# Fused attention and gated FFN: where the QKV projection leaves PSUM, and where q and k are scaled

## The chip, the cores and the metric

One Trainium2 chip, one core. The metric is the time of one execution on the device in microseconds; lower is better. Engines are named as in the profile: PE (TensorE, PEld its weight loads), DVE (VectorE), ACT (ScalarE), POOL (GpSimd), SP (SyncE, which issues the DMAs here). Columns are elements of the free dimension of a tile of 128 partitions.

## The reference

Input x is 2 x 1024 x 512 in float32. All of it is float32:

```python
xn = layernorm(x)                       # no weights
q, k, v = xn @ Wq.T, xn @ Wk.T, xn @ Wv.T    # 32 q heads, 8 k/v heads, head size 128
q, k = rmsnorm(q) * q_norm_w, rmsnorm(k) * k_norm_w    # over the head's 128 elements
scores = q @ k.T / sqrt(128) + slope[head] * (key - query), masked to key <= query
s = softmax(scores) @ v, all heads side by side, @ Wo.T
g = silu(down(silu(gate(xn)) * up(xn)))      # inner size 1376
out = x + s * g
```

Four q heads share one k/v head (G = 4).

## The kernel before, in words

A **unit** is one batch and one k/v head: 2 x 8 = 16 units, in order, the function `units`. A unit has 8 row tiles of 128 tokens. PE keeps float32 accuracy by splitting each operand into a high and a low part (`_hi`, `_lo`, type float32r) and adding three products, so whatever PE multiplies is first copied by ACT (the high part) and then subtracted by DVE or POOL (the low part).

Within a unit the work goes in steps i = 0 to 7 (the last unit of a batch has two more that drain the pipeline). In step i, PE's order is written out by hand in `step` (L366): project tile i + 2 (`project`, L288), the output projection of tile i - 2 (`out_project`, L354), then slots k = 0, 1, ... Each slot may hold: one block of the scores of tile i (`scores`, L314, up to 512 keys of one head, 4 to 8 blocks per step), one turn of the probabilities of tile i - 1 through the transpose ring (`turn_probs`, L329), one weighing of v by a turned block (`weigh`, L340, two slots behind its turn), and after the last turn the transposes of q and k of tile i + 1 (`turn_q`, `turn_k`). The numbers of turns in steps 0 to 7 are 8, 1, 2, ... 7; those of score blocks are 4 in steps 0 to 3 and 8 in steps 4 to 7. The other engines have functions of the same form, in the same order of steps and slots. Every engine takes its own queue in order; semaphores tie them, with counts per tile (`tile(U, i)` = U*8 + i + 1), per score block and per ring entry.

PSUM has 8 banks: the projection takes two (`qkv_ps`), scores two (`score_ps`), the ring three (`ring_ps`), one is `out_ps`. The projection of one tile is 128 x 768 columns: 512 of q (bank one), 128 of k and 128 of v (bank two), as 12 pairs of a 512-column and a 256-column matmul (L299, L300). What happens to it:

- ACT squares q and k (`square`, L479, 640 columns out of PSUM, to `qk_sq`), then copies v to `v_nat` (`stage_v`, L485, 128 columns).
- DVE sums the squares per head (`sum_squares`, L643).
- POOL computes the inverse roots, 12 small dependent operations and one multiply (`norms`, L905, to `rq`, 5 numbers per token), then splits v (`split_v`, L915). In step 1 it makes the low part of the output weights between the two (`low_o`, L878, two operations of 1024 columns), in step 5 that of the next unit's QKV weights (`low_w`, L872, four of 768 columns, whose high parts ACT copies in slots 0 to 3 of that step, `high_w`).
- DVE multiplies q and k by `rq`, from PSUM into `natural` (`scale_qk`, L650), in slot k = 2 of the step. One operation, 640 columns.
- PE turns the result in the next step.

The two banks are free for the next projection only after v is copied and q and k are scaled: L291 and L292 wait for both. In the first steps of a batch the tiles 0 and 2 are projected into the score banks (`first_ps`), and the scores of step 1 wait for the same two (L379, L380).

DVE's slot is: `bias` of score block k (L668), `low_probs` of turn k (L685), then `scale_qk` if k is 2, then the low parts of q and k. A score block n waits until the bias of block n - 2 is done (two score banks). A step of DVE begins with `low_att` (L700), which the output projection waits for, `divide` (L691), `sum_squares` and `add_y` (L705). Output projection 2 of a unit waits besides for the first half of `o_lo` at head 0 and for the second at head 2 (L358, L359).

Of the kernel before, what the change touches and what calls it, by code (L numbers as in the profile page):

```python
# [33 lines left out]
VBUFS = 4  # L34
# [27 lines left out]
LAG = 2  # L62

# [18 lines left out]
def build(nc, x, w_qkv, w_o, w_ffn, q_norm, k_norm, rel, slopes, inv_slopes, ident_in, out):  # L82
    ctx = ExitStack()
    with ctx:
# [69 lines left out]
        qk_done, v_staged, v_high, v_split = sem("qk_done"), sem("v_staged"), sem("v_high"), sem("v_split")  # L154
# [28 lines left out]
        def tile(U, i):  # L183

            return U * TILES + i + 1

# [94 lines left out]
        def _(pe):  # L281
# [6 lines left out]
            def project(U, i, acc, early):  # L288

                if not early:  # L290
                    pe.wait_ge(qk_done, tile(U, i) - 1)  # L291
                    pe.wait_ge(v_staged, tile(U, i) - 1)  # L292
                for c in range(DC):
                    if i == 0:
                        pe.wait_ge(w_split, U * DC + c + 1)
                    for xT, w in ((xT_hi, qkv_hi), (xT_hi, qkv_lo), (xT_lo, qkv_hi)):
                        a = xT[:, c, i * P:(i + 1) * P]
                        go, end = c == 0 and xT is xT_hi and w is qkv_hi, c == DC - 1 and xT is xT_lo
                        pe.matmul(acc[:, 0:BANK], a, w[:, c, 0:D], start=go, stop=end)  # L299
                        mm = pe.matmul(acc[:, BANK:BANK + KV], a, w[:, c, D:NW], start=go, stop=end)  # L300
                mm.then_inc(projected, 1)

            def turn_q(U, i, r, first, t):
                ring_free(U, r, first)
                pe.wait_ge(qk_done, t)
                for h in range(G):
                    tr = pe.transpose(ring_ps[:, ring_bank(r), h * P:(h + 1) * P], qk[i % 2][:, h * P:(h + 1) * P], ident[:, :])  # L307
                tr.then_inc(ring_full, 1)

            def turn_k(U, i, r, first):  # L310
                ring_free(U, r, first)
                pe.transpose(ring_ps[:, ring_bank(r), 0:P], qk[i % 2][:, G * P:NQK], ident[:, :]).then_inc(ring_full, 1)  # L312
# [53 lines left out]
            def step(U, i, first, last):  # L366
                ahead = not (last and i >= TILES - 1)
                if first and i == 0:
# [6 lines left out]
                    turn_k(U, 1, RING_AT[0] + BEFORE[0] + 1, True)  # L375
# [13 lines left out]
                for k in range(slots):  # L389
# [8 lines left out]
                    if ahead and turns and k == turns + 1:  # L398
                        turn_q(U, (i + 1) % TILES, RING_AT[i] + BEFORE[i], first, tile(U, i + 1))
                        turn_k(U, (i + 1) % TILES, RING_AT[i] + BEFORE[i] + 1, first)  # L400
# [14 lines left out]
            for b in range(B):  # L415
# [41 lines left out]
                def unit(U, first, last):  # L457
                    if first:
# [8 lines left out]
                        turn_k(U, 0, 1, True)  # L467
# [10 lines left out]
        def _(act):  # L478
            def square(acc, t, first):  # L479
                act.wait_ge(projected, t)  # L480
                if not first:
                    act.wait_ge(summed, t - 1)
                act.activation(qk_sq, acc[:, 0:(G + 1) * P], ACT.Square).then_inc(squared, 1)  # L483

            def stage_v(acc, i, t, early):  # L485
                if not early:
                    act.wait_ge(v_split, t - VBUFS)
                act.activation(v_nat[:, i % VBUFS, :], acc[:, BANK + P:BANK + KV], ACT.Copy).then_inc(v_staged, 1)

# [50 lines left out]
            for b in range(B):  # L540
# [17 lines left out]
                def step(U, i, first, last):  # L558
                    ahead = not (last and i >= TILES - 1)
                    if first and i == 0:  # L560
# [4 lines left out]
                        square(first_ps, tile(U, 2), False)  # L565
                        stage_v(first_ps, 2, tile(U, 2), True)
                        high_o(U, 0, False)
                        high_o(U, 1, False)
                        square(qkv_ps, tile(U, 3), False)
                        stage_v(qkv_ps, 3, tile(U, 3), True)  # L570
# [7 lines left out]
                    if not (last and i >= TILES - 2) and not (first and i == 1):  # L578
                        square(qkv_ps, tile(U, i + 2), False)
                        stage_v(qkv_ps, (i + 2) % TILES, tile(U, i + 2), False)  # L580
# [20 lines left out]
                def unit(U, first, last):  # L601
                    if first:
                        square(first_ps, tile(U, 0), True)
                        stage_v(first_ps, 0, tile(U, 0), True)
                        for t in range(HT, TILES):
                            high_x(b, t)
                        square(qkv_ps, tile(U, 1), False)
                        stage_v(qkv_ps, 1, tile(U, 1), True)
# [33 lines left out]
        def _(dve):  # L642
            def sum_squares(t, first):  # L643
# [3 lines left out]
                dve.tensor_reduce(sq_sum[:, :], qk_sq.rearrange("p (g n) -> p g n", g=G + 1),  # L647
                                  AX.X, ALU.add).then_inc(summed, 1)
# [100 lines left out]
            for b in range(B):  # L749
                def step(U, i, first, last):  # L750
                    ahead = not (last and i >= TILES - 1)
                    if first and i == 0:
                        for k in range(G):
                            bias(U, 0, k)
                        scale_qk(qkv_ps, 1, tile(U, 1))
# [3 lines left out]
                        scale_qk(first_ps, 0, tile(U, 2))  # L759
# [20 lines left out]
                    for k in range(slots):  # L780
# [8 lines left out]
                        if k == 2 and not (last and i >= TILES - 2):  # L789
                            scale_qk(qkv_ps, (i + 2) % TILES, tile(U, i + 2))  # L790
# [4 lines left out]
                def unit(U, first, last):  # L795
                    if first:
# [4 lines left out]
                        scale_qk(first_ps, 0, tile(U, 0))  # L801
# [38 lines left out]
        def _(pool):  # L840
# [53 lines left out]
            for b in range(B):  # L894
# [111 lines left out]
```

## Time and profile before

| | us |
|---|---|
| median of 3 runs | 2518.57 (2516.94 to 2519.94) |
| the profiled execution, its time | 2519.08 |
| its span in the profile | 2517.3 |
| PE busy in the span | 2443.9 |
| DVE busy | 1692.9 |
| ACT busy | 1233.5 |
| POOL busy | 782.9 |

The mean granted clock of TensorE was 0.993 of full speed. DMA moved 92.33 MB, 37 GB/s on average. How to read the rows: a row of a timeline has the start, the duration, the engine, the line of the kernel, the operation and its tiles; x4 says that four like it were merged into one row; the bracket tells how long the engine had been idle before it and what ended that. Matmuls are pipelined: each starts before the one ahead has ended, so the distance of two starts is what one costs. A row of the groups has busy time and the mean in ns, then the idle time ahead of them.

### The profile page before, as it was taken

The numbers are of one execution on the slowest core, as the hardware profiler recorded it, in microseconds if no ns is written. First come the engines' busy times: TensorE is split into PE (matmuls) and PEld (weight loads), VectorE is DVE, ScalarE is ACT, GpSimd is POOL, SyncE is SP. The second block draws the span as 40 slices with busy tenths as digits, with TensorE's granted clock in tenths as the row PEclk, the third lists the DMA queues.
The fourth block names the chain that finished last, engine by engine and source line by source line (L and its number), as shares of the span: only waits on it lengthen the run. The fifth ranks groups of instructions, "written<-read, shape, count | busy, mean of one in ns | idle before, by whom it ended". The sixth has DMA issues, their size and how long they took to land. (4 is left out here: it accounts for less than half of the span.)

```text
span 2517.3 us, 39632 instructions
## 1 busy us (share of the span) xinstructions
PE 2443.9 (97%) x13232; PEld 2070.5 (82%) x13232; DVE 1692.9 (67%) x3709; ACT 1233.5 (49%) x2548; POOL 782.9 (31%) x2154
## 2 busy tenths in 40 slices
PE   5999999999999999999989999999999999998998
PEld 4888888888888888788878888888888888887887
DVE  5777777786877777823257777777777777777132
ACT  3545555454545554543345455555554555545333
POOL 3313132322322323244433232323241313231443
PEclk8999999999999999999989999999999999999999
DMA  2000000000000000023320101000000000010223
GB/s 110 18 26 18 26 18 26 18 26 18 26 18 26 18 8 36 26 76 134 109 76 1 43 1 36 8 26 18 26 17 26 18 26 18 1 43 9 93 90 111
DMA packets 22858, 92.33 MB, mean 37 GB/s; under 512 B 6528, under 2 KB 6656, under 8 KB 18560
## 3 DMA queue, kind: packets, MB, share of 16 engines
q1 hardware_dynamic: 22656, 89.80, 10.3%
q8 instruction: 106, 1.74, 0.3%
q14 instruction: 96, 0.79, 0.1%
HBM read 85.60 MB, written 4.19 MB: 36 GB/s over the span
## 5 line engine op out<-in xcount | busy, mean ns | idle before, releaser
L511 ACT ACTIVATE pT_hi<-ring_ps 128x512 fp32r<-128x512 f32 x576 | 343.7, 599 | 547.3 <-PE ring_ps L336 536.2
L688 DVE TENSOR_TENSOR pT_lo<-ring_ps,pT_hi 128x512 fp32r<-128x512 f32 x576 | 394.4, 688 | 66.9 <-ACT pT_hi L511 63.3
L503 ACT ACTIVATE probs<-probs,low_min 128x896 f32<-128x896 f32 (+7 forms) x512 | 394.9, 773 | 53.9 <-DVE low_min L680 53.8
L680 DVE CUSTOM_DVE_ANT_0 probs<-score_ps,rel_sb,slope 128x512 f32<-128x512 f32 (+3 forms) x512 | 329.1, 645 | 27.6 <-PE score_ps L325 14.5
L336 PE MATMUL ring_ps<-ident,probs 128*128 128x128 f32 x2304 | 346.8, 274 | 0.7 <-DVE probs L698 0.7
L850 POOL TENSOR_SCALAR rs_x<-sq_sum 128x5 f32<-128x5 f32 x128 | 25.5, 199 | 1014.5 <-DVE sq_sum L647 945.2
L336 PEld LDWEIGHTS ring_ps<-ident,probs 128*128 128x128 f32 x2304 | 278.1, 140 | 51.0 <-issue 1.3
L325 PE MATMUL score_ps<-kv_hi,qT_hi 128*128 128x512 f32 (+3 forms) x768 | 283.1, 369 | 15.5 <-DVE natural L653 8.4
L349 PE MATMUL out_ps<-pT_hi,kv_hi 128*128 128x512 f32 x576 | 266.3, 462 | 3.1 <-DVE pT_lo L688 2.7
L325 PE MATMUL score_ps<-kv_hi,qT_lo 128*128 128x512 f32 (+3 forms) x768 | 268.0, 349 | 0.0
L325 PE MATMUL score_ps<-kv_lo,qT_hi 128*128 128x512 f32 (+3 forms) x768 | 266.1, 347 | 0.0
L698 DVE TENSOR_SCALAR probs<-probs,rec 128x896 f32<-128x896 f32 (+7 forms) x512 | 243.2, 538 | 4.5
L483 ACT ACTIVATE natural<-qkv_ps 128x640 f32<-128x640 f32 x124 | 87.6, 706 | 302.8 <-PE qkv_ps L300 302.8
L349 PE MATMUL out_ps<-pT_hi,kv_lo 128*128 128x512 f32 x576 | 227.1, 394 | 0.0
L349 PE MATMUL out_ps<-pT_lo,kv_hi 128*128 128x512 f32 x576 | 225.6, 392 | 0.0
L299 PE MATMUL qkv_ps<-qkv_hi,xT_hi 128*128 128x512 f32 x496 | 200.3, 404 | 17.8 <-DVE natural L653 17.8
L361 PE MATMUL out_ps<-o_hi,attT_hi 128*128 128x512 f32 x512 | 202.8, 396 | 6.8 <-DVE attT_lo L702 6.8
L361 PE MATMUL out_ps<-o_hi,attT_lo 128*128 128x512 f32 x512 | 201.3, 393 | 0.0
L361 PE MATMUL out_ps<-o_lo,attT_hi 128*128 128x512 f32 x512 | 200.5, 392 | 0.0
L299 PE MATMUL qkv_ps<-qkv_lo,xT_hi 128*128 128x512 f32 x496 | 196.4, 396 | 0.0
L299 PE MATMUL qkv_ps<-qkv_hi,xT_lo 128*128 128x512 f32 x496 | 196.3, 396 | 0.0
L325 PEld LDWEIGHTS score_ps<-kv_hi,qT_hi 128*128 128x128 f32 x768 | 146.1, 190 | 43.5 <-DVE natural L653 9.0
(135 smaller groups left out, 5306.2 us busy)
## 6 DMA issues: line engine op xcount, KB each, us to landing
qkv_raw<-w_ffn_dram SPq DMA_DIRECT2D x44, 768.0 KB, 4.2
qkv_raw<-w_qkv_dram SPq DMA_DIRECT2D x16, 1536.0 KB, 6.8
o_raw<-w_o_dram SPq DMA_DIRECT2D x16, 1024.0 KB, 4.8
probs<-x_dram SPq DMA_DIRECT2D x4, 1024.0 KB, 7.2
o_raw<-x_dram SPq DMA_DIRECT2D x4, 1024.0 KB, 6.8
out_dram<-y SPq DMA_DIRECT2D x16, 256.0 KB, 3.7
rel_sb<-rel_dram SPq DMA_DIRECT2D x1, 512.0 KB, 11.4
inv_slope<-inv_slopes_dram SPq DMA_DIRECT2D x16, 2.5 KB, 1.6
```

The source lines that it names most:

```text
L299: pe.matmul(acc[:, 0:BANK], a, w[:, c, 0:D], start=go, stop=end)
L325: mm = pe.matmul(score_ps[:, n % 2, 0:hi - lo], q[:, i % 2, h * P:(h + 1) * P], kt[:, lo:hi], start=(q is qT_hi and kt is kT_hi), stop=(q ...
L336: tr = pe.transpose(ring_ps[:, ring_bank(r), h * P:(h + 1) * P], probs[p % 2][:, h, j * P:(j + 1) * P], ident[:, :])
L349: mm = pe.matmul(out_ps[:, :], v[:, j * P:(j + 1) * P], pt[:, slot, :], start=(j == 0 and v is v_hi and pt is pT_hi), stop=(j == turns - 1 ...
L361: mm = pe.matmul(out_ps[:, :], a[:, h * P:(h + 1) * P], w[:, h * D:(h + 1) * D], start=(h == 0 and a is attT_hi and w is o_hi), stop=(h == ...
L483: act.activation(qk_sq, acc[:, 0:(G + 1) * P], ACT.Square).then_inc(squared, 1)
L503: act.activation(row, row, ACT.Exp, scale=-1.0, bias=low_min[:, i % 2, h, HEAD_CHUNKS[i] - 1:HEAD_CHUNKS[i]], accum_out=row_sum[:, i % 2, ...
L511: act.activation(pT_hi[:, n % SLOTS, :], ring_ps[:, ring_bank(r), :], ACT.Copy).then_inc(ring_high, 1)
L680: dve.tensor_tensor_reduce(out=probs[i % 2][:, h, lo:hi], in0=score_ps[:, n % 2, 0:hi - lo], in1=rel_sb[:, at:at + hi - lo], scale=slope[: ...
L688: dve.tensor_tensor(out=pT_lo[:, n % SLOTS, :], in0=ring_ps[:, ring_bank(r), :], in1=pT_hi[:, n % SLOTS, :].bitcast(F32), op=ALU.subtract) ...
L698: dve.tensor_scalar(row, row, rec[:, h:h + 1], None, ALU.mult).then_inc(divided, 1)
L850: chained(pool.tensor_scalar(xx, src, mul, add, ALU.mult, ALU.add), done, 1)
```

## The change

ScalarE now copies all 768 columns of the projection to SBUF, into one of three buffers, behind the squares. The PSUM banks are given back when that copy is done (`unloaded`), which is all that the next projection waits for. VectorE scales q and k in place in SBUF. POOL splits v out of the same buffer, and the copy waits until the v of three tiles before is split. The scaling moves from slot 2 to slot 3 (slot 4 in step 3). The projection's matmuls stay 512 + 256 columns.

```diff
-VBUFS = 4
+NBUFS = 3
+SCALE_AT = [3, 3, 3, 4, 3, 3, 3, 3]
...
-        natural = sb("natural", [P, 3 * NQK])
-        qk = [natural[:, k * NQK:(k + 1) * NQK] for k in range(2)]
-        qk_sq = natural[:, 2 * NQK:3 * NQK]
-        v_nat = sb("v_nat", [P, VBUFS, P])
+        natural, qk_sq = sb("natural", [P, NBUFS, NW]), sb("qk_sq", [P, NW])
...
+        def qk_of(t):
+            return natural[:, (t - 1) % NBUFS, 0:NQK]
+        def v_of(t):
+            return natural[:, (t - 1) % NBUFS, NQK:NW]
...
                 if not early:
-                    pe.wait_ge(qk_done, tile(U, i) - 1)
-                    pe.wait_ge(v_staged, tile(U, i) - 1)
+                    pe.wait_ge(unloaded, tile(U, i) - 1)
...
                 if first and i == 1:
-                    pe.wait_ge(qk_done, tile(U, 2))
-                    pe.wait_ge(v_staged, tile(U, 2))
+                    pe.wait_ge(unloaded, tile(U, 2))
...
-            def square(acc, t, first):
+            def unload(acc, t, first):
                 act.wait_ge(projected, t)
                 if not first:
                     act.wait_ge(summed, t - 1)
-                act.activation(qk_sq, acc[:, 0:(G + 1) * P], ACT.Square).then_inc(squared, 1)
-
-            def stage_v(acc, i, t, early):
-                if not early:
-                    act.wait_ge(v_split, t - VBUFS)
-                act.activation(v_nat[:, i % VBUFS, :], acc[:, BANK + P:BANK + KV], ACT.Copy).then_inc(v_staged, 1)
+                act.activation(qk_sq[:, 0:NQK], acc[:, 0:NQK], ACT.Square).then_inc(squared, 1)
+                if t > NBUFS:
+                    act.wait_ge(v_split, t - NBUFS)
+                act.activation(natural[:, (t - 1) % NBUFS, :], acc[:, 0:NW], ACT.Copy).then_inc(unloaded, 1)
...
-            def scale_qk(acc, i, t):
+            def scale_qk(t):
                 dve.wait_ge(rq_done, t)
-                dve.wait_ge(v_staged, t)
-                dve.tensor_tensor(out=qk[i % 2].rearrange("p (g n) -> p g n", g=G + 1),
-                                  in0=acc[:, 0:(G + 1) * P].rearrange("p (g n) -> p g n", g=G + 1),
+                dve.wait_ge(unloaded, t)
+                dve.tensor_tensor(out=qk_of(t).rearrange("p (g n) -> p g n", g=G + 1),
+                                  in0=qk_of(t).rearrange("p (g n) -> p g n", g=G + 1),
                                   in1=rq[:, :].unsqueeze(2).to_broadcast([P, G + 1, P]), op=ALU.mult).then_inc(qk_done, 1)
...
-                        if k == 2 and not (last and i >= TILES - 2):
-                            scale_qk(qkv_ps, (i + 2) % TILES, tile(U, i + 2))
+                        if k == SCALE_AT[i % TILES] and not (last and i >= TILES - 2):
+                            scale_qk(tile(U, i + 2))
...
-                    pool.wait_ge(v_staged, tile(U, i))
-                    split(v_hi[:, i * P:(i + 1) * P], v_lo[:, i * P:(i + 1) * P], v_nat[:, i % VBUFS, :], v_high, tile(U, i), v_split)
+                    pool.wait_ge(unloaded, tile(U, i))
+                    split(v_hi[:, i * P:(i + 1) * P], v_lo[:, i * P:(i + 1) * P], v_of(tile(U, i)), v_high, tile(U, i), v_split)
```

The calls of `square` and `stage_v` become calls of `unload` at the same places, and the transposes of q and k read `qk_of(t)`.

## Rows read from the trace of the kernel before

**Rows 1.** The page, busy time, share of the span and instructions, PE

```profile
PE 2443.9 (97%) x13232; PEld 2070.5 (82%) x13232; DVE 1692.9 (67%) x3709; ACT 1233.5 (49%) x2548; POOL 782.9 (31%) x2154
```

**Rows 2.** Waits of PE: waiting line, releaser, us in total, times, longest

```profile
PE qkv_ps L299 <- DVE natural L653: 17.8, 16, 1.3
PE score_ps L325 <- DVE natural L653: 8.4, 2, 4.3
```

**Rows 3.** Timeline of PE, unit 1: start of step 1, its end, start of step 2

```profile
180.84 0.40 PE L299 MATMUL qkv_ps<-qkv_hi,xT_hi 128*128 128x512 f32 x1
...
185.06 0.40 PE L361 MATMUL out_ps<-o_hi,attT_hi 128*128 128x512 f32 x1
...
191.30 0.28 PE L325 MATMUL score_ps<-kv_hi,qT_lo 128*128 128x256 f32 x1
192.72 0.50 PE L299 MATMUL qkv_ps<-qkv_hi,xT_hi 128*128 128x512 f32 x1 [1.14 <-DVE natural L653]
193.05 0.28 PE L300 MATMUL qkv_ps<-qkv_hi,xT_hi 128*128 128x256 f32 x1
```

**Rows 4.** Timeline of DVE, the same stretch

```profile
192.58 0.74 DVE L659 SCALAR_TENSOR_TENSOR qT_lo<-ring_ps,wcol,qT_hi 128x512 fp32r<-128x512 f32 x1
...
193.44 0.47 DVE L680 CUSTOM_DVE_ANT_0 probs<-score_ps,rel_sb,slope 128x256 f32<-128x256 f32 x1
...
195.07 0.69 DVE L702 TENSOR_TENSOR attT_lo<-out_ps,attT_hi 128x512 fp32r<-128x512 f32 x1 [1.15 <-ACT attT_hi L516]
```

**Rows 5.** Timeline of ACT, the same stretch and the turn behind it

```profile
191.72 0.67 ACT L492 ACTIVATE qT_hi<-ring_ps,wcol 128x512 fp32r<-128x512 f32 x1
...
193.95 0.51 ACT L503 ACTIVATE probs<-probs,low_min 128x256 f32<-128x256 f32 x1 [0.42 <-DVE low_min L680]
...
194.46 0.58 ACT L516 ACTIVATE attT_hi<-out_ps 128x512 fp32r<-128x512 f32 x1
...
200.91 0.60 ACT L511 ACTIVATE pT_hi<-ring_ps 128x512 fp32r<-128x512 f32 x1 [2.85 <-PE ring_ps L336]
```

**Rows 6.** Groups by line and shape: DVE with two operands, ACT's squares

```profile
L817 DVE TENSOR_TENSOR pT_lo<-probs,pT_hi 128x512 fp32r<-128x512 f32 x44 | 30.5, 693 | 30.8 <-ACT pT_hi L621 30.8
L815 DVE TENSOR_TENSOR probs<-qkv_ps,probs 128x512 f32<-128x512 f32 x44 | 30.4, 691 | 216.9 <-ACT probs L617 216.9
...
L483 ACT ACTIVATE natural<-qkv_ps 128x640 f32<-128x640 f32 x124 | 87.6, 706 | 302.8 <-PE qkv_ps L300 302.8
```

**Rows 7.** Timelines of POOL and DVE in the FFN of batch 0

```profile
1181.81 2.40 POOL L897 TENSOR_TENSOR kv_lo<-qkv_raw,kv_hi 128x1024 fp32r<-128x1024 f32 x1
1189.30 1.32 POOL L902 TENSOR_TENSOR qT_lo<-qkv_raw,qT_hi 128x512 fp32r<-128x512 f32 x1 [5.09 <-ACT qT_hi L556]
1190.59 2.83 POOL L897 TENSOR_TENSOR kv_lo<-qkv_raw,kv_hi 128x1024 fp32r<-128x1024 f32 x1
...
1189.51 1.67 DVE L834 TENSOR_TENSOR y<-y,o_raw 128x512 f32<-128x512 f32 x1
```

**Rows 8.** Timeline of POOL, unit 1, step 1: the low part of o

```profile
191.76 4.75 POOL L881 TENSOR_TENSOR o_lo<-o_raw,o_hi 128x1024 fp32r<-128x1024 f32 x2
```

**Rows 9.** Timeline of DVE, unit 1, step 5, slots 2 to 4

```profile
246.75 0.81 DVE L653 TENSOR_TENSOR natural<-qkv_ps,rq 128x640 f32<-128x640 f32 x1
...
248.22 0.69 DVE L688 TENSOR_TENSOR pT_lo<-ring_ps,pT_hi 128x512 fp32r<-128x512 f32 x1 [0.20 <-ACT pT_hi L511]
248.83 0.74 DVE L680 CUSTOM_DVE_ANT_0 probs<-score_ps,rel_sb,slope 128x512 f32<-128x512 f32 x1
```

**Rows 10.** Timeline of PE, unit 1, step 5: the seventh score block

```profile
249.84 0.40 PE L325 MATMUL score_ps<-kv_hi,qT_hi 128*128 128x512 f32 x1
```

**Rows 11.** Timeline of POOL, unit 1, step 5: the low part of the weights

```profile
246.03 7.28 POOL L875 TENSOR_TENSOR qkv_lo<-qkv_raw,qkv_hi 128x768 fp32r<-128x768 f32 x4
```

**Rows 12.** Timeline of DVE, unit 0, step 7, a bias

```profile
157.61 0.81 DVE L680 CUSTOM_DVE_ANT_0 probs<-score_ps,rel_sb,low_min 128x512 f32<-128x512 f32 x1 [0.20 <-PE score_ps L325]
```

**Rows 13.** Timeline of PE, unit 0, step 1: the first turn of probabilities

```profile
57.55 1.09 PE L336 MATMUL ring_ps<-ident,probs 128*128 128x128 f32 x4 [0.53 <-DVE probs L698]
```

More of the change, by code:

```diff
@@ L299, in project @@
                         pe.matmul(acc[:, 0:BANK], a, w[:, c, 0:D], start=go, stop=end)
-                        mm = pe.matmul(acc[:, BANK:BANK + KV], a, w[:, c, D:NW], start=go, stop=end)
+                        mm = pe.matmul(acc[:, BANK:NW], a, w[:, c, D:NW], start=go, stop=end)
                 mm.then_inc(projected, 1)
@@ L374, in step @@
                     turn_q(U, 1, RING_AT[0] + BEFORE[0], True, tile(U, 1))
-                    turn_k(U, 1, RING_AT[0] + BEFORE[0] + 1, True)
+                    turn_k(U, 1, RING_AT[0] + BEFORE[0] + 1, True, tile(U, 1))
                     project(U, 3, qkv_ps, True)
@@ L399, in step @@
                         turn_q(U, (i + 1) % TILES, RING_AT[i] + BEFORE[i], first, tile(U, i + 1))
-                        turn_k(U, (i + 1) % TILES, RING_AT[i] + BEFORE[i] + 1, first)
+                        turn_k(U, (i + 1) % TILES, RING_AT[i] + BEFORE[i] + 1, first, tile(U, i + 1))
                     if 0 <= k - LAG < turns:
@@ L466, in unit @@
                         turn_q(U, 0, 0, True, tile(U, 0))
-                        turn_k(U, 0, 1, True)
+                        turn_k(U, 0, 1, True, tile(U, 0))
                     for i in range(TILES + 2 if last else TILES):
@@ L564, in step @@
                         high_k(U, 1, RING_AT[0] + BEFORE[0] + 1)
-                        square(first_ps, tile(U, 2), False)
-                        stage_v(first_ps, 2, tile(U, 2), True)
+                        unload(first_ps, tile(U, 2), False)
                         high_o(U, 0, False)
                         high_o(U, 1, False)
-                        square(qkv_ps, tile(U, 3), False)
-                        stage_v(qkv_ps, 3, tile(U, 3), True)
+                        unload(qkv_ps, tile(U, 3), False)
                         return
@@ L578, in step @@
                     if not (last and i >= TILES - 2) and not (first and i == 1):
-                        square(qkv_ps, tile(U, i + 2), False)
-                        stage_v(qkv_ps, (i + 2) % TILES, tile(U, i + 2), False)
+                        unload(qkv_ps, tile(U, i + 2), False)
                     chunks, turns, slots = shape_of_step(i, first)
@@ L602, in unit @@
                     if first:
-                        square(first_ps, tile(U, 0), True)
-                        stage_v(first_ps, 0, tile(U, 0), True)
+                        unload(first_ps, tile(U, 0), U == 0)
                         for t in range(HT, TILES):
                             high_x(b, t)
-                        square(qkv_ps, tile(U, 1), False)
-                        stage_v(qkv_ps, 1, tile(U, 1), True)
+                        unload(qkv_ps, tile(U, 1), False)
                         high_q(U, 0, 0)
@@ L754, in step @@
                             bias(U, 0, k)
-                        scale_qk(qkv_ps, 1, tile(U, 1))
+                        scale_qk(tile(U, 1))
                         low_q(U, 1, RING_AT[0] + BEFORE[0])
@@ L758, in step @@
                         sum_squares(tile(U, 2), False)
-                        scale_qk(first_ps, 0, tile(U, 2))
+                        scale_qk(tile(U, 2))
                         sum_squares(tile(U, 3), False)
@@ L800, in unit @@
                             low_x(b, t)
-                        scale_qk(first_ps, 0, tile(U, 0))
+                        scale_qk(tile(U, 0))
                         sum_squares(tile(U, 1), False)
```

10 lines of the change are left out of this document (5 added, 5 removed).

## The prediction

> **What bounds the kernel.** I read the busy shares first: PE is busy 97% of the span [rows 1]. So only two things can change the time: PE's idle stretches, and work that becomes late enough to make new ones. The waits come next. The largest repeated one stands before the projection, on the scaling of q and k, 16 times, 17.8 us in all: at most 1.3 and on average 1.1 us, once in each of the 16 units (batch x key head). The other wait on that scaling, 8.4 us, comes twice, at the start of a batch [rows 2]. The timelines show where the first sits. As the 16 are so alike, one unit can be read for all, and I use unit 1 (the second). Its step 1 has only four score blocks and one turn of probabilities, so PE reaches the projection of step 2 before VectorE has scaled the tile projected in step 1. PE starts its last score matmul at 191.30 and the projection at 192.72 [rows 3].
>
> **What leaves.** A pair of projection matmuls (512 and 256 columns) takes 4.22 / 12 = 0.35 us, so the 256-column one has 0.12 and the 512-column one 0.23 [rows 3]. The gap of 1.42 is thus 1.30 of stall, of which the wait's row shows 1.14, and the matmul behind it comes after 0.33 in place of 0.23, as its weights were not loaded ahead. A stall costs 0.26 more than its idle row says: 17.8 + 16 x 0.26 = 22.0 us. In the new kernel the projection waits only for ScalarE's copy of the tile before, made some 5 us earlier. All 22.0 go.
>
> **What is late next, step 1 to 2.** PE would start the projection at 191.42 and the output projection at 195.64. That needs the low half of the attention tile (L702), which hangs on ScalarE: q's copy from 191.72 [rows 5], then on VectorE q's and k's low parts and the last bias. Before, the scaling stood ahead of them, and q's low part began at 192.58; now it begins when q's copy is done, near 192.40, so the last bias, the exponential (193.95), the attention copy (194.46) and L702 (195.07) all come 0.18 earlier [rows 4, 5]. L702 takes 0.69 and ends at 195.58; PE starts at 195.63 at the best and loses the 0.10 of a late weight load. I take 0.1 for it.
>
> **The scaling gets a second SBUF operand.** It read PSUM and SBUF, now it reads SBUF twice. Its own time stays: the same operation on 512 columns takes 691 ns with PSUM and 693 with both in SBUF [rows 6], so 0.82 us. The Trainium skill (VectorE: DVE Perf Modes, the section on the TRN2 errata) gives SBUF sources 62 cycles less fixed cost than PSUM sources; that would be 0.06 us per scaling, an estimate from that page, and the rows do not show it.
> But such an operation collides with GpSimd. L834 (two SBUF operands) took 1.67 us, not 0.69, where it was issued at 1189.51 into a GpSimd operation of 1189.30 to 1190.62, and ended 0.56 behind its end. GpSimd's next, back to back, came out at 1193.42, 2.24 behind L834's end and 0.43 longer than the 2.40 of the one before it: VectorE was let in between the two [rows 7]. I take that as the rule: the scaling waits for the end of the running GpSimd operation and ends 0.56 + 128 columns (0.13) = 0.69 behind it. The Trainium skill (SBUF — State Buffer, "Who interferes with whom") says the same against this change: a VectorE instruction with two SBUF inputs and a GpSimd one that reads SBUF exclude each other for a whole instruction; by that rule the trace agrees.
> In step 1 the scaling now follows the last bias, near 193.7, within o's low part (two operations from 191.76, 4.75 together, first end 194.14 [rows 8]). It ends at 194.83, just ahead of L702. The second ends 2.24 later, at 197.07. Output projection 2 waits for it at its third head, due 195.74 + 6 x 0.235 = 197.15. Nothing to 0.2: I take 0.1. So of 22.0 us, 16 x 0.2 = 3.2 come back: **gain 18.8**.
>
> **Step 5, the new wait.** The scaling moves from slot 2 to slot 3. In step 5 VectorE waits for ScalarE before the low part of turn 3 (248.22), as ScalarE also copies the next unit's weights there. Before, the scaling (246.75) filled that gap; now the gap is empty, and it comes behind, at 248.83, where the fifth bias was. That bias was done at 249.58 and PE's seventh score block, which needs it, began at 249.84 [rows 9, 10]. Without any collision the scaling would end at 249.65, the bias at 249.57 + 0.75 = 250.32, PE go on at 250.38: a stall of 0.54 + 0.10. With it: GpSimd splits the next weights, four operations in 7.28 from 246.03, with ends at 247.85 and 249.67 [rows 11]. The scaling ends at 250.36, the bias at 251.03, PE starts at 251.09: 1.25 + 0.10 = **1.35 us in each of 15 units** (the last has no next weights), 20.2 us. Nothing of that kind waits behind it, so it is not regained. In the other steps VectorE catches up in the slots behind (it waits for PE again in step 7, 0.20 in a slot [rows 12]) and GpSimd runs nothing long, so I cost their move at nothing; a slip of some 0.5 us in one of them would reach PE, and without that cover each step would pay it.
>
> **The wider copy.** 640 columns take 706 ns [rows 6]; 768 take between that and 706 x 768/640 = 847, against 0.27 for V alone: 0.44 to 0.58 more, 128 times, up to 74 us of ScalarE's time. It stands behind the squares, where ScalarE then waited 2.85 us for PE [rows 5]; without that cover it would cost as much. In step 2 it also waits for V's split behind o's low part, near 197.9, and is done near 198.8; the next copy is due at 200.91 - 1.2 = 199.7. Queued behind that wait are only the turns' copies. SP's loads hang on the weights' split, 0.7 later and needed tens of us after: nothing.
>
> **Start of a batch.** PE no longer waits 4 us before the first scores. But the first turn of probabilities waits for the division, which on VectorE still stands behind that scaling: PE started it at 57.55, after a wait of 0.53 [rows 13]. The wait moves there whole; gain 0, at most 8.4.
>
> **The sum.** -18.8 + 20.2 = +1.4 us on the profiled execution's 2519.08, which is 0.5 above the median of 2518.57: **2520.0 us**. A measurement of this kernel tells about 0.2%, 5 us, from no change.
>
> **Rivals.**
> Collisions do not reach the scaling (its second operand is only five numbers, spread out). Then step 1 gives 22.0 - 1.6 and step 5 costs 0.64 x 15 = 9.6: -10.8, 2508 us. For it: no row shows a spread operand. Against: L834 and its like. 0.20.
> Step 5 has room I do not see, as ScalarE's order or an earlier fourth bias might bring the turn forward: -18.8, 2500 us. Against: the copy at 248.22 is bound by ScalarE's queue. 0.14.
> Slower: GpSimd keeps its turn between back-to-back operations. It decides as soon as the scaling meets such a pair. Step 1: release 196.51, L702 done 197.81, output projection 2.33 late against 1.40 won; step 5: release 253.31, the bias at 254.67, PE 4.99 late. 16 x 0.93 + 15 x 4.99 = +90, 2608 us. For it: in each step it would meet such a pair. Against: GpSimd's lengthened operation in rows 7. 0.06.
>
> **Chances.** My forecast has 0.60. Its own spread: each unit's balance is 1.2 won and 1.35 lost, either uncertain by 0.3, so 2513 to 2528; of the 0.60, 0.42 lie within 5 us, 0.14 above, 0.04 below. With the rivals: faster 0.38, same 0.42, slower 0.20. The range 2505 to 2528 leaves out the last rival, most of the second and the forecast's tail.
>
> **What would show it.** In the new profile the wait of the projection on L653 is gone and the projection follows the scores of step 1 without a gap. The output projection of step 2 shows a wait of a few tenths on L702 or on o's split. In step 5 the seventh score block waits 1 to 1.2 us for the bias, 15 times. The scaling takes 0.82 us in most steps, about 1.15 in step 1 and 1.5 in step 5. Wrong would be: no wait in step 5 (then 2500), 0.5 there with every scaling at 0.82 (2508), or scalings of 3 to 5 us (2608).

## The result and the profile after

| | before | after |
|---|---|---|
| median, us (16 runs each, side by side) | 2518.08 (2516.94 to 2521.32) | 2521.76 (2519.75 to 2525.17) |
| the profiled execution, its time | 2519.08 | 2521.61 |
| its span | 2517.3 | 2519.8 |
| mean granted clock | 0.993 | 0.992 |

The ratio is 1.0016, with a 95% interval of 1.0009 to 1.0022: 3.7 us slower, by less than the 0.2% that the prediction called no change. The ratios of the experiments are each against runs of the kernel before beside them: 11 with a median of 2518.64 us for e1 to e4, 15 with 2519.47 for e5 to e8. Differences between experiments are those of their medians. The medians of the kernel before lie up to 1.4 us apart (2518.08, 2518.64, 2519.47), so a difference across these sets, such as e1 against the change or e8 against e1, is uncertain by about as much.

The page of the changed kernel, the row that answers to [rows 1]:

```profile
PE 2446.0 (97%) x13232; PEld 2067.3 (82%) x13232; DVE 1725.6 (68%) x3709; ACT 1302.0 (52%) x2548; POOL 806.7 (32%) x2154
```

The other engines work more and PE's share is the same. What PE waits for has changed in two places. Waits of PE (line, releaser, us in total, times, longest), to be read against [rows 2]; L330 is the scores, L341 the turn of probabilities, L677 the bias, L695 the division:

```profile
PE score_ps L330 <- DVE low_min L677: 17.3, 18, 1.1
PE ring_ps L341 <- DVE probs L695: 10.0, 2, 5.2
```

The 17.8 us ahead of the projection are gone, and 17.3 us ahead of the scores are there. The 8.4 us at the two starts of a batch have become 10.0 on another line. PE's timeline in unit 1 shows the first, at the end of step 1, against [rows 3], and in step 5, against [rows 10]:

```profile
192.35 0.28 PE L330 MATMUL score_ps<-kv_hi,qT_lo 128*128 128x256 f32 x1
192.47 0.40 PE L304 MATMUL qkv_ps<-qkv_hi,xT_hi 128*128 128x512 f32 x1
...
196.71 0.50 PE L366 MATMUL out_ps<-o_hi,attT_hi 128*128 128x512 f32 x1
...
250.97 0.50 PE L330 MATMUL score_ps<-kv_hi,qT_hi 128*128 128x512 f32 x1 [1.05 <-DVE low_min L677]
251.31 0.39 PE L330 MATMUL score_ps<-kv_lo,qT_hi 128*128 128x512 f32 x1
```

The projection starts 0.12 behind the last score matmul, where it was 1.42. The seventh score block waits 1.05 in its place, and the matmul behind it starts 0.34 later instead of 0.23. Now VectorE's timeline in the same two places, against [rows 4, 9] (L650 is the scaling, L685 the low part of a turn, L699 the low part of the attention tile):

```profile
194.33 0.48 DVE L677 CUSTOM_DVE_ANT_0 probs<-score_ps,rel_sb,slope 128x256 f32<-128x256 f32 x1
...
194.73 1.15 DVE L650 TENSOR_TENSOR natural<-natural,rq 128x640 f32<-128x640 f32 x1
195.97 0.69 DVE L699 TENSOR_TENSOR attT_lo<-out_ps,attT_hi 128x512 fp32r<-128x512 f32 x1
...
196.78 2.61 DVE L695 TENSOR_SCALAR probs<-probs,rec 128x256 f32<-128x256 f32 x4
...
248.13 0.69 DVE L685 TENSOR_TENSOR pT_lo<-ring_ps,pT_hi 128x512 fp32r<-128x512 f32 x1 [0.94 <-ACT pT_hi L513]
248.74 1.50 DVE L650 TENSOR_TENSOR natural<-natural,rq 128x640 f32<-128x640 f32 x1
250.17 0.74 DVE L677 CUSTOM_DVE_ANT_0 probs<-score_ps,rel_sb,slope 128x512 f32<-128x512 f32 x1
```

And GpSimd's beside them, against [rows 8, 11]:

```profile
192.79 5.34 POOL L878 TENSOR_TENSOR o_lo<-o_raw,o_hi 128x1024 fp32r<-128x1024 f32 x2
...
245.90 7.84 POOL L872 TENSOR_TENSOR qkv_lo<-qkv_raw,qkv_hi 128x768 fp32r<-128x768 f32 x4
```

In step 1 the first GpSimd operation takes 2.40 (half of 4.75 is 2.38, and L897 took 2.40 [rows 7, 8]) and ends at 195.19; the scaling ends at 195.88, 0.69 behind it. In step 5 each of the four takes 7.28 / 4 = 1.82, the second ends at 249.54, and the scaling ends at 250.24, 0.70 behind it. GpSimd pays too: 5.34 for 4.75, 7.84 for 7.28. One more operation of VectorE is longer, which the prediction did not have: the four divisions of step 1's probabilities (L695) take 2.61 in place of 1.88, as GpSimd's second operation, late by then, is still running (to 198.13). Where it is over before they start, in unit 1 of e6 below, the four take 1.14. In unit 1 no wait of PE comes of that. In step 5 VectorE has 0.94 us of nothing ahead of turn 3, and behind it the scaling stands in the way of the bias.

### The profile page after: what moved, and what is told of

Its sections match the earlier page's. It is cut to its first block and busy times, and to the rows that moved or that the text cites. A ratio compares the mean times of both kernels' runs of the same rounds, so it can differ in the third digit from the quotient of the medians.

```text
span 2519.8 us, 39525 instructions
## 1 busy us (share of the span) xinstructions
PE 2446.0 (97%) x13232; PEld 2067.3 (82%) x13232; DVE 1725.6 (68%) x3709; ACT 1302.0 (52%) x2548; POOL 806.7 (32%) x2154
## 5 line engine op out<-in xcount | busy, mean ns | idle before, releaser
L685 DVE TENSOR_TENSOR pT_lo<-ring_ps,pT_hi 128x512 fp32r<-128x512 f32 x576 | 395.7, 688 | 84.4 <-ACT pT_hi L513 80.1
L341 PE MATMUL ring_ps<-ident,probs 128*128 128x128 f32 x2304 | 346.8, 274 | 10.0 <-DVE probs L695 10.0
L677 DVE CUSTOM_DVE_ANT_0 probs<-score_ps,rel_sb,slope 128x512 f32<-128x512 f32 (+3 forms) x512 | 329.0, 645 | 28.8 <-PE score_ps L330 11.9
L341 PEld LDWEIGHTS ring_ps<-ident,probs 128*128 128x128 f32 x2304 | 278.0, 140 | 60.0 <-issue 10.4
L330 PE MATMUL score_ps<-kv_hi,qT_hi 128*128 128x512 f32 (+3 forms) x768 | 284.4, 370 | 24.7 <-DVE low_min L677 17.3
L354 PE MATMUL out_ps<-pT_hi,kv_hi 128*128 128x512 f32 x576 | 266.6, 463 | 2.8 <-DVE pT_lo L685 2.6
L330 PE MATMUL score_ps<-kv_hi,qT_lo 128*128 128x512 f32 (+3 forms) x768 | 267.7, 349 | 0.0
L330 PE MATMUL score_ps<-kv_lo,qT_hi 128*128 128x512 f32 (+3 forms) x768 | 266.2, 347 | 0.0
L695 DVE TENSOR_SCALAR probs<-probs,rec 128x896 f32<-128x896 f32 (+7 forms) x512 | 255.7, 563 | 4.5
L487 ACT ACTIVATE qk_sq<-qkv_ps 128x640 f32<-128x640 f32 x124 | 87.6, 706 | 285.4 <-PE qkv_ps L305 285.4
L354 PE MATMUL out_ps<-pT_hi,kv_lo 128*128 128x512 f32 x576 | 227.2, 394 | 0.0
L354 PE MATMUL out_ps<-pT_lo,kv_hi 128*128 128x512 f32 x576 | 226.0, 392 | 0.0
L330 PEld LDWEIGHTS score_ps<-kv_hi,qT_hi 128*128 128x128 f32 x768 | 146.0, 190 | 58.2 <-DVE low_min L677 27.7
```

The lines of the kernel that those rows point to most:

```text
L330: mm = pe.matmul(score_ps[:, n % 2, 0:hi - lo], q[:, i % 2, h * P:(h + 1) * P], kt[:, lo:hi], start=(q is qT_hi and kt is kT_hi), stop=(q ...
L354: mm = pe.matmul(out_ps[:, :], v[:, j * P:(j + 1) * P], pt[:, slot, :], start=(j == 0 and v is v_hi and pt is pT_hi), stop=(j == turns - 1 ...
L487: act.activation(qk_sq[:, 0:NQK], acc[:, 0:NQK], ACT.Square).then_inc(squared, 1)
L677: dve.tensor_tensor_reduce(out=probs[i % 2][:, h, lo:hi], in0=score_ps[:, n % 2, 0:hi - lo], in1=rel_sb[:, at:at + hi - lo], scale=slope[: ...
L685: dve.tensor_tensor(out=pT_lo[:, n % SLOTS, :], in0=ring_ps[:, ring_bank(r), :], in1=pT_hi[:, n % SLOTS, :].bitcast(F32), op=ALU.subtract) ...
L695: dve.tensor_scalar(row, row, rec[:, h:h + 1], None, ALU.mult).then_inc(divided, 1)
```

## The experiments

The first six ask about the forecast's terms, the last two about the wait at the start of a batch and about what the early release of the banks is for.

### e1: the scaling of step 5 moved to slot 7

```diff
-SCALE_AT = [3, 3, 3, 4, 3, 3, 3, 3]
+SCALE_AT = [3, 3, 3, 4, 3, 7, 3, 3]
```

> The changed kernel, with the scaling of step 5 in slot 7, behind the last bias. My theory: the new wait of 1.05 us before the seventh score block (1.35 with its late weights), once in each of 15 units, is all that eats the gain. In slot 7 the scaling ends before the attention tile's low part is due, so the wait goes and nothing takes its place: 2521.8 - 15 x 1.35 = 2501.5 us, 0.993 of the kernel before. Rival, the gain never came, and the 1.05 us would be waited for anyway by something behind it (the wider copy, or o's split): the time stays near 2521 and a wait of about 1 us appears elsewhere in each unit.

Measured: 2503.22 us, ratio 0.9937 (0.9925 to 0.995). Against the change as it stands that is 18.5 us. PE's wait on the bias, and the scaling where it stands now:

```profile
PE score_ps L330 <- DVE low_min L677: 0.7, 2, 0.4
```

```profile
253.94 0.99 DVE L650 TENSOR_TENSOR natural<-natural,rq 128x640 f32<-128x640 f32 x1
```

The 15 waits of step 5 are gone with their whole price, and no other wait took their place. So the loss of the change lies in this one operation, and what is left is its gain, 0.63%.

### e2: the scaling of step 5 back in slot 2, where it was

```diff
-SCALE_AT = [3, 3, 3, 4, 3, 3, 3, 3]
+SCALE_AT = [3, 3, 3, 4, 3, 2, 3, 3]
```

> The changed kernel, with the scaling of step 5 back in slot 2, so that in step 5 only its operands differ from the kernel before. By the theory that a scaling with two SBUF operands waits for the end of GpSimd's running operation: it is issued at 246.65 in unit 1, within the first split of the weights (245.90 to 247.72), ends near 248.4 (a duration of about 1.75 us), the low part of turn 3 ends near 249.5 instead of 248.82, and PE stands 0.5 to 0.65 us before a weighing: 2521.8 - 15 x (1.35 - 0.6) = 2510.5 us. By the rival that only the slot matters: the scaling takes 0.82 us, no wait in step 5, 2501.5 us.

Measured: 2510.99 us, ratio 0.9969 (0.9957 to 0.998). From VectorE's timeline and PE's waits:

```profile
244.57 1.78 DVE L650 TENSOR_TENSOR natural<-natural,rq 128x640 f32<-128x640 f32 x1
```

```profile
PE score_ps L330 <- DVE low_min L677: 1.7, 8, 0.3
```

Here the scaling runs into the first of the four GpSimd operations and takes 1.78. It costs 7.8 us against e1 (2510.99 - 2503.22), although PE's row shows little of it. The rest is in delays too short for that row. The idle time ahead of PE's weight loads in unit 1 shows them, before the sixth score block and before the next weighing:

```profile
246.87 0.19 PEld L330 LDWEIGHTS score_ps<-kv_hi,qT_hi 128*128 128x128 f32 x1 [0.52 <-DVE low_min L677]
...
247.47 0.19 PEld L354 LDWEIGHTS out_ps<-pT_hi,kv_hi 128*128 128x128 f32 x1 [0.18 <-DVE pT_lo L685]
```

PE is 0.25 and 0.13 late at these two, and each costs another 0.10 by its late weight load: 0.58 in this unit, where the expectation had one wait of 0.5 to 0.65. The slot is the old one, so I take this as the price of the collision alone. That slot 2 costs nothing in SBUF without a collision was not tried.

### e3: the kernel before, with its scaling of step 5 in slot 3

```diff
-                        if k == 2 and not (last and i >= TILES - 2):
+                        if k == (3 if i == 5 else 2) and not (last and i >= TILES - 2):
```

> The kernel before, with the scaling of step 5 in slot 3 and nothing else changed: it still reads PSUM. Theory: the slot alone costs 0.54 + 0.10 us in each of 15 units, as the bias behind it comes late for the seventh score block: 2518.1 + 9.6 = 2527.7 us, and the scaling takes 0.82 us. By the rival that the whole wait in the changed kernel is the collision with GpSimd, the time stays at 2518; by the one that it is all the slot, it grows by 20 us to 2538.

Measured: 2527.31 us, ratio 1.0036 (1.0023 to 1.0048), some 9 us slower than before. PE's wait on the bias and VectorE's scaling (L653, out of PSUM):

```profile
PE score_ps L325 <- DVE low_min L680: 5.9, 17, 0.4
```

```profile
249.11 0.81 DVE L653 TENSOR_TENSOR natural<-qkv_ps,rq 128x640 f32<-128x640 f32 x1
```

With the operand in PSUM the scaling takes 0.81 beside the same GpSimd operations. This is the price of the slot without the collision: 8.7 us by 2527.31 - 2518.64, 0.58 in each of 15 units.

### e4: the GpSimd operations of step 5 cut short

```diff
-                    pool.tensor_tensor(out=qkv_lo[:, c, :], in0=qkv_raw[:, c, :], in1=qkv_hi[:, c, :].bitcast(F32),
+                    n = NW if U == 0 else 8
+                    pool.tensor_tensor(out=qkv_lo[:, c, 0:n], in0=qkv_raw[:, c, 0:n], in1=qkv_hi[:, c, 0:n].bitcast(F32),
```

> The changed kernel, with GpSimd's low part of the weights in step 5 cut from 768 to 8 columns in each of its four operations (the rest of the low part is left stale from the first unit, so part of the computation is left out). GpSimd is then free when the scaling comes. Theory: the scaling of step 5 takes 0.82 us, the wait before the seventh score block falls from 1.05 to about 0.35 and 15 x 0.70 = 10.5 us go: 2511 us. By the rival that the collision plays no part, the wait and the time stay.

Measured: 2510.12 us, ratio 0.9966 (0.9954 to 0.9979).

```profile
PE score_ps L330 <- DVE low_min L677: 6.3, 18, 0.4
```

```profile
247.74 0.82 DVE L650 TENSOR_TENSOR natural<-natural,rq 128x640 f32<-128x640 f32 x1
```

The same kernel as the changed one, but with nothing to collide with: the scaling is back at 0.82, the wait falls from 1.05 to at most 0.4, and 11.6 us are regained. The idle time of VectorE ahead of turn 3 stays (0.93), so that wait has nothing to do with the collision.

### e5: ScalarE's copy made twice

```diff
+                act.wait_ge(again_done, t - 1)
+                act.activation(again[:, :], acc[:, 0:NW], ACT.Copy).then_inc(again_done, 1)
                 act.activation(natural[:, (t - 1) % NBUFS, :], acc[:, 0:NW], ACT.Copy).then_inc(unloaded, 1)
```

> The changed kernel, in which ScalarE makes its copy of 768 columns twice for each tile (the first into a buffer that nobody reads). Theory: the copy lies in ScalarE's idle time before the turns, so another 128 x 0.81 = 104 us of ScalarE's busy time cost PE nothing in the steps; at the start of a batch up to 0.8 us each: 2521.8 to 2523.5 us. Rival, the wider copy is what holds the changed kernel back (each tile's copy delays the first turn): the second copy costs some tenths in each of 124 steps, 2540 us or more.

Measured: 2521.69 us, ratio 1.001 (1.0001 to 1.0019), against 2521.76 without the second copy. The two copies in the groups (busy time, mean ns of one, then the idle time ahead of them):

```profile
L492 ACT ACTIVATE again<-qkv_ps 128x768 f32<-128x768 f32 x124 | 100.2, 808 | 29.3 <-POOL kv_lo L870 29.3
L493 ACT ACTIVATE natural<-qkv_ps 128x768 f32<-128x768 f32 x124 | 101.0, 815 | 0.0
```

The second copy is another 100 us of ScalarE's time, more than the 68.5 that the change added (1233.5 to 1302.0), and the run's time does not move. So the wider copy, and the release of the banks 0.81 us later that the second one brings, cost nothing that these runs can show (11 of them, from 2518.90 to 2524.61).

### e6: the scaling of step 1 put ahead, in slot 2

```diff
-SCALE_AT = [3, 3, 3, 4, 3, 3, 3, 3]
+SCALE_AT = [3, 2, 3, 4, 3, 3, 3, 3]
```

> The changed kernel, with the scaling of step 1 in slot 2, where the kernel before had it. By the collision theory it is issued near 192.9 in unit 1, just behind the start of the first operation of o's low part (192.79 to 195.17), ends near 195.9 (a duration near 3 us), and q's low part, the last bias, the exponential and the attention tile's low part come behind it: the output projection starts near 199.0 instead of 196.7, 2.3 us in each of 16 units, 2559 us. By the rival that a spread second operand does not collide: the scaling takes 0.82 us and the output projection is on time or 0.3 us late, 2522 to 2527 us.

Measured: 2569.81 us, ratio 1.0201 (1.0187 to 1.0215): 48.0 more than the changed kernel. VectorE's scaling and PE's wait in unit 1, then the same place two units on:

```profile
194.66 3.00 DVE L650 TENSOR_TENSOR natural<-natural,rq 128x640 f32<-128x640 f32 x1 [0.90 <-POOL rq L910]
```

```profile
PE out_ps L366 <- DVE attT_lo L699: 40.7, 20, 2.3
```

```profile
200.81 0.50 PE L366 MATMUL out_ps<-o_hi,attT_hi 128*128 128x512 f32 x1 [2.20 <-DVE attT_lo L699]
...
466.24 0.79 PE L366 MATMUL out_ps<-o_hi,attT_hi 128*128 128x512 f32 x1 [2.25 <-DVE attT_lo L699]
466.83 0.63 PE L366 MATMUL out_ps<-o_lo,attT_hi 128*128 128x512 f32 x1
```

```profile
200.80:204.00 3.20, 3.19 (x14) 2.69 (x15) 2.05 (x7) 0.71 (x1) 0.60 (x3) 1.00 0.89 317
466.20:470.20 4.00, 3.96 (x11) 3.15 (x12) 1.93 (x6) 0.73 (x1) 0.99 (x5) 0.59 0.73 262
```

The last two rows are windows right behind those waits (length, busy time of PE, PEld, DVE, ACT and POOL, then the granted clock, DMA's share and GB/s). The scaling here waits for the same number `rq` that GpSimd has just made, so both start together and the scaling stands behind the whole first operation: 194.58 + 2.40 + 0.69 = 197.67, and it ends at 197.66. The wait it makes was expected. What was missed is the clock. The waits on L699 grew by 40.7 - 6.8 = 33.9. The granted clock fell from 0.992 to 0.987: (1 - clock) times the span is 33.4 us against 20.2, so 13.2 us more that PE did not get. 33.9 + 13.2 = 47.1 of the 48.0. The clock is given to 0.001, so its part is good to some 2 us.

### e7: e1, and the division of a batch's first step put ahead of the scaling

```diff
-                        scale_qk(tile(U, 2))
-                        sum_squares(tile(U, 3), False)
...
+                    if first and i == 2:
+                        scale_qk(tile(U, 3))
...
+                        if first and i == 1 and k == 0:
+                            scale_qk(tile(U, 2))
+                            sum_squares(tile(U, 3), False)
-                        if k == SCALE_AT[i % TILES] and not (last and i >= TILES - 2):
+                        if k == SCALE_AT[i % TILES] and not (first and i == 1) and not (last and i >= TILES - 2):
```

> The kernel with the scaling of step 5 in slot 7, in which the first step of a batch is reordered besides: VectorE divides the probabilities before it waits for the scaling of tile 2, and scales tile 3 only at the start of step 2. PE's stall of 4.9 and 5.2 us before the first turn breaks up: turn 0 and a score block go before it, and the next wait is that of the transposes of q for the scaling of tile 2, some 3 us. Gain 2 to 4 us per batch; if the granted clock, which was at 1.2 GHz for some 5 us behind that stall, then stays at 2.4, another 2 us each: 2503.2 - 4 to 12, so about 2496 us. Rival: the ScalarE copy of tile 3, which waits for v's split, holds the first turn's copy in ScalarE's queue, and the gain is under 2 us in all.

Measured: 2501.57 us, ratio 0.993 (0.9917 to 0.9944). That is the lowest median of all, but its interval and that of e1 (0.9925 to 0.995) overlap, so the two cannot be told apart. PE's waits:

```profile
PE ring_ps L312 <- DVE natural L650: 9.2, 4, 2.8
PE out_ps L354 <- DVE pT_lo L685: 5.8, 7, 1.6
```

The wait of 10.0 us on the division is gone, as meant. But the tiles that were scaled late are now turned late: waits of 1.8 us before L312 in e1 are 9.2 now, and those before L354 went from 2.9 to 5.8. In the start of the second batch 5.2 us of one wait became 2.8 + 1.6. ScalarE's timeline there:

```profile
1291.80 0.81 ACT L490 ACTIVATE natural<-qkv_ps 128x768 f32<-128x768 f32 x1 [4.00 <-POOL kv_lo L870]
...
1292.51 0.59 ACT L513 ACTIVATE pT_hi<-ring_ps 128x512 fp32r<-128x512 f32 x1
```

The forecast of 2496 us missed, and the rival held, in size (1.7 us against e1) and in this row: the copy of tile 3 waits 4.00 us for v of tile 0 to be split, as both use one buffer, and the copy of the first turn, which PE had made by 1288, stands behind it in ScalarE's queue. The wait of 2.8 before it is on the scaling, which waits for GpSimd's `rq`. Whether a fourth buffer, with which that copy need not wait, would bring the gain was not tried. The clock did not stay up either: behind the two waits it was at 0.50 again (matmuls of 0.63 us from 1294.54 on).

### e8: e1, and PE waits for the scaling again before it projects

```diff
                     pe.wait_ge(unloaded, tile(U, i) - 1)
+                    pe.wait_ge(qk_done, tile(U, i) - 1)
```

> The kernel with the scaling of step 5 in slot 7, in which the projection waits again for the scaling of the tile before, besides the copy, as before the change: the copy is there, the early release of the banks is not. Theory: the whole gain is that release. In unit 1 the scaling of step 1, held by o's low part, ends at 195.88, and the projection starts there and not at 192.47: 3.5 us in each of 16 units, and a tenth or two behind steps 2 and 3: 2503.2 + 54 = 2557 us (2550 to 2575). Rival, the gain comes from fewer waits on PE or from the scaling's other operand: 2503 to 2525 us.

Measured: 2625.37 us, ratio 1.0422 (1.0407 to 1.0436): 122 more than e1, where 54 were expected. PE's waits, and the timeline and two windows behind one of them:

```profile
PE qkv_ps L305 <- DVE natural L651: 59.5, 32, 3.4
PE qkv_ps L305 <- issue: 27.6, 14, 2.0
```

```profile
201.57 0.77 PE L305 MATMUL qkv_ps<-qkv_hi,xT_hi 128*128 128x512 f32 x1 [3.35 <-DVE natural L651]
```

```profile
201.50:206.80 5.30, 5.23 (x16) 4.49 (x17) 3.31 (x6) 0.03 (x1) 2.91 (x3) 0.50 0.34 111
206.80:212.00 5.20, 5.20 (x30) 4.45 (x29) 1.60 (x3) 1.41 (x2) 0.99 (x5) 1.00 0.21 88
```

The wait of step 2 is there 16 times with up to 3.4 us, as expected. The other 16 of the row are of 0.4 to 0.6 us in front of step 3, where a tenth or two was expected. Two things were left out. The wait on the slot-7 scaling of step 5 holds up the projection of step 6 by 2.0 in 14 units: the profile puts it down to issue, but in unit 1 that scaling ends at 266.21 and the projection starts at 266.31. And the clock: 0.979 against 0.991 in e1, (1 - clock) times the span 55.1 us against 22.5, so 32.6 us. 59.5 + 27.6 + 32.6 = 119.7 of the 122, again good to some 2 us.

## Why the prediction was right

It gave 2520.0 us, and 2521.76 was measured; no change was its likeliest case. The forecast is the difference of two terms of some 20 us, and each can be read by itself. e1 has the gain without the loss. Three timelines give PE's projection at the start of step 2, first in unit 1, then in unit 2; in the changed kernel it is 192.47 in unit 1, in the one before 192.72 [rows 3]. Before, then after, then e1:

```profile
322.19 0.50 PE L299 MATMUL qkv_ps<-qkv_hi,xT_hi 128*128 128x512 f32 x1 [1.15 <-DVE natural L653]
```

```profile
322.19 0.40 PE L304 MATMUL qkv_ps<-qkv_hi,xT_hi 128*128 128x512 f32 x1
```

```profile
193.26 0.40 PE L304 MATMUL qkv_ps<-qkv_hi,xT_hi 128*128 128x512 f32 x1
...
321.63 0.40 PE L304 MATMUL qkv_ps<-qkv_hi,xT_hi 128*128 128x512 f32 x1
```

This unit takes 129.47 us before, 129.72 after and 128.37 in e1: 1.10 is won in it and 1.35 lost. In the kernel before it is one of the shortest: the units range from 129.47 to 129.79. The table has the same distance, from the projection of step 2 to that of the next unit, as the mean over units 1 to 6 and 9 to 14. In these units the clock was at its full level in all six traces.

| us per unit | before | the change | e1 | e2 | e3 | e4 |
|---|---|---|---|---|---|---|
| mean of 12 | 129.61 | 129.77 | 128.41 | 129.07 | 130.22 | 129.03 |

So 1.20 is won in a unit and 1.37 lost, where the forecast had 1.18 and 1.35. That is closer than the 0.3 which the prediction gave either of them, and that much is luck; the terms below agree one by one.

**What leaves.** Right in an ordinary unit: the gap of 1.42 before the projection is 0.12, the 1.30 of the forecast.

**What is late next, step 1 to 2.** Right in kind and in size: a stall's 1.30 and its late weight load of 0.1 leave and 0.2 was to come back, 1.18 net over the 16. PE reached the output projection 4.24 behind the start of the projection (192.47 to 196.71), 0.02 over 12 x 0.352, with its weights loaded late: 0.50 long and 0.34 to the next start, not 0.23. That is the 0.1 of the first part. VectorE is the reason, as forecast: the low part of the attention tile was ready at 196.66. The third head, which waits for o's low part, starts at 198.22, and its next matmul comes 0.30 behind in place of 0.23. Together these are 0.02 + 0.11 + 0.07 = 0.20.

**The first unit of each batch.** Here the step of the gain failed, in size. I multiplied one unit's stall by 16, and [rows 2] give only the mean. In unit 8 the stall before was 0.50 us, and the changed kernel loses part of it again at once. PE in unit 8, the kernel before, then the changed one:

```profile
1307.16 0.50 PE L299 MATMUL qkv_ps<-qkv_hi,xT_hi 128*128 128x512 f32 x1 [0.50 <-DVE natural L653]
...
1319.34 0.39 PE L299 MATMUL qkv_ps<-qkv_hi,xT_hi 128*128 128x512 f32 x1
```

```profile
1308.43 0.40 PE L304 MATMUL qkv_ps<-qkv_hi,xT_hi 128*128 128x512 f32 x1
...
1317.97 0.44 PE L330 MATMUL score_ps<-kv_hi,qT_hi 128*128 128x384 f32 x1 [0.44 <-DVE low_min L677]
...
1321.21 0.40 PE L304 MATMUL qkv_ps<-qkv_hi,xT_hi 128*128 128x512 f32 x1
```

From one projection to the next it takes 12.18 before and 12.78 after, 0.60 back where the forecast had 0.2 in all; against a stall of 0.50 + 0.26 that unit gives 0.2. VectorE is late there: the scaling (2.15 us) meets GpSimd's first operation soon after its start, the four divisions take 2.79 in place of 1.88, and the bias that PE waits for ends 9.48 behind the projection in place of 8.51. (Unit 0, with a stall of 1.29 before, also depends on the first loads and was not taken apart.)

**The granted clock.** The forecast has no term for it. e1's gain as measured is 2518.64 - 2503.22 = 15.4 us; the forecast had 18.8, and 14 units at 1.20 alone are 16.8. The two traces show where it stays. From step 2 of unit 0 to that of unit 7, and from unit 8 to unit 15, e1 is 16.5 us shorter, yet its span only 15.1. In the first 70 us the granted clock was 0.90 before and 0.83 in e1, which is 70 x 0.07 = 4.9 us of PE's time. It was 0.85 in the changed kernel and 0.90 in e2, though e1, e2 and the change do not differ up to there, so this is not shown to come from the change. The result has it too: of the changed kernel's 16 runs the eight with a mean clock of 0.993 took 2519.75 to 2521.79 us, the five with 0.991 took 2523.86 to 2525.17. The mean of the 16 is 0.9922, that of the 11 runs of the kernel before beside e1 is 0.9929. Times the span these are 1.8 us, so about half of the 3.7 us by which the change is slower may be clock.

**The collision.** Right, and the step on which all hung. The scaling with a spread second operand excludes GpSimd as one with two full tiles does, and it is let in between two back-to-back operations: in the changed kernel's trace the 31 scalings that met one of the long operations (16 in step 1, 15 in step 5, 1.15 to 2.15 us) all ended 0.68 behind the end of the running one, where the forecast had 0.69. By the Trainium skill (SBUF — State Buffer, "Who interferes with whom") two SBUF inputs on VectorE and a GpSimd read of SBUF exclude each other; by that rule the trace agrees. e2, e3 and e4 take the loss of step 5 apart:

| scaling of step 5 | out of PSUM | in SBUF | in SBUF, GpSimd's work cut |
|---|---|---|---|
| slot 2 | 2518.6 (before) | 2511.0 (e2) | not tried |
| slot 3 | 2527.3 (e3) | 2521.8 (the change) | 2510.1 (e4) |
| slot 7 | not tried | 2503.2 (e1) | not tried |

The collision costs 7.8 us in slot 2 (e2 against e1) and 11.6 in slot 3 (the change against e4); the slot by itself costs 8.7 (e3). By the means of 12 units the collision in slot 3 costs 0.75 (the forecast had 0.71), in slot 2 0.66, and the slot 0.61 out of PSUM (e3) and 0.62 in SBUF (e4 against e1), where the forecast had 0.64. Together the forecast had 20.2, and 15 units at 1.37 are 20.5; the medians give 18.5, and e1's trace has some 2 us more of lower clock than the changed kernel's ((1 - clock) times the span is 22.5 against 20.2). Both parts were needed: either alone would have left the change faster than before, as e2 and e4 are.

**The wider copy.** Right, shown by e5. It takes 809 ns (rows below), within the bounds of 0.71 and 0.85 us. In step 2 it waited 1.40 for v's split, as foreseen, and was done at 199.82: the forecast's 198.8, plus the 1.03 by which GpSimd's work lies later in this trace (192.79 for 191.76). ScalarE's timeline and its group, in the changed kernel:

```profile
199.01 0.81 ACT L490 ACTIVATE natural<-qkv_ps 128x768 f32<-128x768 f32 x1 [1.40 <-POOL kv_lo L867]
200.82 0.60 ACT L513 ACTIVATE pT_hi<-ring_ps 128x512 fp32r<-128x512 f32 x1 [1.00 <-PE ring_ps L341]
```

```profile
L490 ACT ACTIVATE natural<-qkv_ps 128x768 f32<-128x768 f32 x124 | 100.3, 809 | 29.2 <-POOL kv_lo L867 29.2
```

**The scaling's own time.** Right: 819 ns in the median of all 128, against some 0.82 with PSUM. The Trainium skill (VectorE: DVE Perf Modes, the section on the TRN2 errata) gives SBUF sources 62 cycles less fixed cost than PSUM sources; no row here shows that.

**Start of a batch.** Right in kind: the wait moves whole to the turn behind the division. It grows, 10.0 us for 8.4, where the forecast had it unchanged. e7 shows that taking it away there gives back too little to measure.

**The rivals.** "Collisions do not reach the scaling" is ruled out by scalings of 1.15 and 1.50, "step 5 has unseen room" by the 15 waits. The third, GpSimd keeping its turn, is ruled out by the same rows. e6 comes closest to it: there one whole GpSimd operation goes first, and the time is 48 us worse.

Three expectations missed. e6 and e8 both lack a term for the granted clock; what sets which of these waits costs the clock stays open. e7 missed because its rival held.

## What to carry to other kernels

When an operation moves from PSUM to SBUF its own duration may stay the same while it gains a new enemy: look at what GpSimd does beside it, at each place where it is issued. When the result is wanted only in the next step, put it where its engine has nothing urgent behind it, here the last slot, and not into the gap where it used to fit. And a change that shows nothing can be a gain and a loss of the same size: one constant for one step out of eight turned this one from 0.2% slower to 0.6% faster.

## What the runs showed of the hardware

- VectorE's scaling, issued together with or into one of GpSimd's operations of 768 or 1024 columns on SBUF, took 1.15, 1.50, 1.78 and 3.00 us in unit 1 (the change, e2, e6) instead of 0.82, and ended 0.68 behind the end of the running GpSimd operation, also where GpSimd had another one ready. One of its operands was five numbers per partition, spread over 640 columns.
- A division with one SBUF operand and one number per partition is held up by GpSimd too: the four of 256 columns took 1.14 us beside no GpSimd operation (e6), 1.88 behind one that ended 0.63 after their start (before), 2.61 behind one that ended 1.35 after it (the change).
- The granted clock can fall behind a short wait of PE, and equal waits are not treated equally. Behind the 15 waits of some 1.05 us in step 5 of the changed kernel it stayed at 1.00. Of the 14 waits of 2.09 to 2.31 us that e6 has in step 2 of its units (without the first of each batch), nine were followed within three matmuls by some of 0.57 to 0.63 us in place of 0.39, which is the level of 1.2 GHz (0.50 granted) instead of 2.4. Of e8's 16 waits there, up to 3.4 us long, six had it at once, four some 1.2 to 1.5 us later (0.74 and 0.75 in two windows), and behind the other six the clock stayed at 1.00. What a fall costs can be read from e8's projections, two after a wait in step 2 and the next ones of the same units:

```profile
216.82 0.47 PE L305 MATMUL qkv_ps<-qkv_hi,xT_hi 128*128 128x512 f32 x1 [0.46 <-DVE natural L651]
...
474.82 0.47 PE L305 MATMUL qkv_ps<-qkv_hi,xT_hi 128*128 128x512 f32 x1 [3.34 <-DVE natural L651]
...
487.68 0.47 PE L305 MATMUL qkv_ps<-qkv_hi,xT_hi 128*128 128x512 f32 x1 [0.44 <-DVE natural L651]
```

From 201.57 to 216.82, with the clock at 0.50 in the first 5.3 us, are 15.25 us; from 474.82 to 487.68, with it whole, 12.86. A wait of 3.35 cost another 2.4.
